# Taking out TensorE's transposes of the identity between the last attention product and the first gate product of a decoder layer

## What is computed

```python
def xattn(input, weight, bias):                 # input is x1, weight is ctx_2048
    x_dq = _fp8_quant_dequant(input)            # scale = 448 / max(abs(x1)), over ALL of x1
    w_dq = _fp8_quant_dequant(weight)
    return jnp.einsum('bmk,bkn->bmn', x_dq, w_dq) + bias

x = layernorm(x + attn(x))                      # x1
x = layernorm(x + xattn(x, ctx, mask))          # x2
x = layernorm(x + ffn(x))                       # silu(x @ gate_w) * (x @ up_w) @ down_w, and experts
```

## Time and profile before

| what | value |
|---|---|
| median of 3 executions | 802.43 us (802.11 to 802.63) |
| the profiled execution's own time | 802.24 us |
| its span, first to last instruction | 800.4 us |
| mean granted TensorE clock over the span | 0.996 |
| PE busy | 778.9 us, 97% of the span |
| DVE busy | 672.9 us, 84% |
| ACT, POOL busy | 317.4 us, 367.6 us |

### The profile page before, as it was taken

The page is one execution under the profiler, slowest core; times in us unless marked ns, Lnnn a source line. Parts: engine busy times, 40 slices in busy tenths (PEclk is TensorE's granted clock), DMA queues, the critical chain, the costliest instruction groups (busy, mean ns, idle before and its releaser), DMA issues. The chain is left out here.

```text
span 800.4 us, 10702 instructions
## 1 busy us (share of the span) xinstructions
PE 778.9 (97%) x3614; PEld 639.1 (80%) x3614; DVE 672.9 (84%) x1334; ACT 317.4 (40%) x696; POOL 367.6 (46%) x300
## 2 busy tenths in 40 slices
PE   8999999999899999999999999999999999999994
PEld 7888888888667878888888888888877877878783
DVE  6887679898889870567699999999999999999997
ACT  6444337365673422222534333333233342333323
POOL 1332122242123311033468767767667667667432
PEclk9999999999999999999999999999999999999998
DMA  8667505635455547001122322322233333322113
GB/s 318 234 146 171 106 9 126 156 89 91 75 132 132 132 119 248 1 1 61 47 62 81 90 74 82 87 81 58 89 110 86 98 84 112 92 65 72 29 53 157
DMA packets 51190, 81.16 MB, mean 101 GB/s; under 512 B 17503, under 2 KB 26463, under 8 KB 50624
## 3 DMA queue, kind: packets, MB, share of 16 engines
q0 software_dynamic: 24240, 32.96, 19.3%
q1 hardware_dynamic: 25312, 47.52, 16.9%
q10 hardware_dynamic: 1584, 0.01, 0.1%
HBM read 110.44 MB, written 12.58 MB: 154 GB/s over the span
## 5 line engine op out<-in xcount | busy, mean ns | idle before, releaser
L1806 PE MATMUL gu<-x_hi,w_hi 128*128 128x512 f32 x516 | 202.1, 392 | 1.8 <-ACT mid L1411 1.8
L1808 PE MATMUL gu<-x_hi,w_lo 128*128 128x512 f32 x516 | 200.8, 389 | 0.0
L1807 PE MATMUL gu<-x_lo,w_hi 128*128 128x512 f32 x516 | 200.8, 389 | 0.0
L1291 POOL TENSOR_TENSOR h_lo<-mid,h_hi 128x512 fp32r<-128x512 f32 x62 | 80.5, 1318 | 103.5 <-ACT h_hi L1417 103.0
L1427 ACT ACTIVATE gates<-dots 128x1 f32<-128x1 f32 x144 | 29.3, 203 | 232.2 <-DVE dots L1663 232.2
L1806 PEld LDWEIGHTS gu<-x_hi,w_hi 128*128 128x128 f32 x516 | 96.9, 188 | 24.0 <-ACT mid L1411 4.3
L1808 PEld LDWEIGHTS gu<-x_hi,w_lo 128*128 128x128 f32 x516 | 96.9, 188 | 20.3
L1807 PEld LDWEIGHTS gu<-x_lo,w_hi 128*128 128x128 f32 x516 | 96.9, 188 | 19.8
L1310 POOL DMA_INDIRECT ctx_q<-table_dram,row_i x64 | 80.3, 1254 | 62.3 <-DVE xall L1672 42.6
L1310 POOL DMA_INDIRECT scratch<-table_dram,row_i x64 | 82.4, 1287 | 39.9 <-issue 23.7
L1572 DVE TENSOR_TENSOR mid<-gu,mid 128x512 f32<-128x512 f32 x64 | 44.1, 690 | 62.3 <-PE gu L1808 41.1
(11 more groups left out here) (249 smaller groups left out, 1446.6 us busy)
## 6 DMA issues: line engine op xcount, KB each, us to landing
stage<-in_ctx SPq DMA_DIRECT2D x7, 1024.0 KB, 6.1
total<-prod POOLq DMA_DIRECT2D x11, 512.0 KB, 4.8
xall<-half_bo POOLq DMA_DIRECT2D x4, 1024.0 KB, 9.9
xhat<-in_L_ffn_gate_w SPq DMA_DIRECT2D x8, 512.0 KB, 3.4
xhat<-in_L_ffn_up_w SPq DMA_DIRECT2D x8, 512.0 KB, 3.4
xall<-in_mask_Bx1xS_ff POOLq DMA_DIRECT2D x4, 1024.0 KB, 10.5
xhat<-in_L_ffn_down_w SPq DMA_DIRECT2D x8, 512.0 KB, 3.4
x_dram<-xall SPq DMA_DIRECT2D x4, 1024.0 KB, 6.9
```

The lines of the kernel that those rows point to most:

```text
L1291: nc.gpsimd.tensor_tensor(lo[:, c], mid[c][:], hi[:, c].bitcast(F32), ALU.subtract).then_inc(hlo_done, 1)
L1806: nc.tensor.matmul(dst, lhs[0], rhs[0], start=start, stop=False)
L1807: nc.tensor.matmul(dst, lhs[0], rhs[1], start=False, stop=False)
L1808: return nc.tensor.matmul(dst, lhs[1], rhs[0], start=False, stop=stop)
```

## The change

All eight groups are taken out, and with them the waits that stood ahead of them. Of the waits, two kinds stay behind in another form: `largest_everywhere` now has a wait for `z_done` of tile 13 (NT - 3), the last reader of its bank `ob2`, ahead of its wait for the diagonal; the waits for `y_scaled`, `minus_first`, `y_done` (TB + 2) and `v3_ready` are gone from this place. No other instruction of any engine changes, and none changes its place.

```diff
@@ first block, PE @@
                 for i in range(TB):
                     attention(LAST, i)
 
-                def keep_running(count):
-
-                    for _ in range(count):
-                        nc.tensor.transpose(ob[3][:, 0:P], ident[:], ident[:])
-
-
-                pe.wait_ge(z_done, NT - 2)
-                keep_running(16)
-                pe.wait_ge(z_done, NT)
-                keep_running(8)
-                pe.wait_ge(x1_done, NT - 1)
-                keep_running(6)
+                pe.wait_ge(z_done, NT - 3)
                 largest_everywhere()
-                keep_running(10)
@@ second block, PE @@
-                def keep_running(bank, count):
-
-                    for _ in range(count):
-                        nc.tensor.transpose(bank[:, 0:P], ident[:], ident[:])
-
-
-                pe.wait_ge(y_scaled, 1)
-                keep_running(ob[3], 5)
                 for i in range(TB):
                     transposes(1, (i,), own_bank, x1t_mm, freed(y_done, 0))
                     cross(0, nothing, (i,))
-                pe.wait_ge(y_done, TB + 2)
-                for i in range(1, TB):
-                    pe.wait_ge(minus_first, i + 1)
-                    keep_running(gu[0], 7)
-                pe.wait_ge(v3_ready, 2)
-                keep_running(gu[0], 4)
                 x2_transposes(0, nothing)
-                keep_running(gu[0], 3)
                 for n in range(TB - 1):
                     gate_up(n, 0, n, 0, 2 if n == 0 else None)
```

## The result

| | kernel before | changed kernel |
|---|---|---|
| median of 20 executions | 802.67 us | 804.66 us |
| lowest to highest | 802.11 to 804.09 us | 802.92 to 809.21 us |
| ratio to before, 95% interval | | 1.0025 (1.0017 to 1.0034) |
| the profiled execution's own time, its span | 802.24, 800.4 us | 805.71, 803.9 us |
| mean granted clock over the span | 0.996 | 0.985 |

A forecast was written before the change was run, and what follows sets the result against it. PE bounds the kernel from the first gate product on, so its delay moves the end. The delay of 0.8 us, with the barrier's -0.2 already in it, on 802.43 gives 803.2 us; range 802.0 to 806.0.

The forecast's parts named there:

- The hidden transposes: The 73 identity transposes hide under the chain of DVE and ACT; their removal costed at nothing, except the ten behind L873.
- some 0.2 us at the barrier: Barrier after L873: without the ten transposes DVE arrives last, 0.20 us sooner: -0.2 us, bounds 0 and 0.49.
- The first fall: Clock halves at about 210.8 or later, cross products start at half speed; 2.4 us lost, 1.44 hidden, +0.8 us at end.
- the bound of +0.25: If L873 already runs at half speed, it ends 0.25 us later, on the chain to the scale: +0.25 us.
- The 4.9 us of slow running: Restart cost read from the program's beginning: 2.4 us lost, at half speed 4.9 us before the clock is up.
- The second fall: Rival: clock falls again, or isn't back, ahead of the gate products; +2.2 on top of +0.8, 805.4 us; chance 0.25.
- each of its gaps is under 4.8 us: Argument against another fall between 220.2 and 228: no gap reaches the idle time after which the clock fell at program's end.
- the share of work: Argument for a fall between 205.96 and 215.19: PE works only an eighth of 9.2 us, nearer to nothing than 44%.
- The likeliest case: One fall of the clock with most of its cost hidden: 803.2 us, within 802.4 to 804.0; chance 0.43.
- the case that had 0.35 against 0.62: Whole kernel slower by a tellable 1.6 us, 804.0 or more: chance 0.35; within that of no change: 0.62.
- Down throughout: Rival: clock stays down from 211 us until the gate products are well under way; +6.8 us, 809 us; chance 0.06.
- The page's rule: Rival from the skill page: transposes don't engage the full clock, so the 73 did nothing; 802.2 us; chance 0.04.

The follow-up runs named there:

- no_ten: The kernel before without only the ten transposes behind L873: 802.31 us against 802.58; the same kernel once more 802.87 against 802.51.
- six: The kernel before with six transposes behind L873 instead of ten: 802.28 us against 802.51, ratio 0.9995.
- second_only: The kernel before without the first block's groups (16, 8, 6, 10), the second block's kept: 802.90 us against 802.58, ratio 1.0000.
- only_sevens: The changed kernel with the three groups of seven back, between cross products and x2 transposes: 803.10 us against before's 802.65, ratio 1.0002.
- first_only: The kernel before without the second block's groups (5, 3 x 7, 4, 3), the first block's kept: 804.47 us against 802.58, ratio 1.0017.
- one_each: The kernel before with one transpose in each place, 10 in all instead of 73, all waits kept: 803.72 us against 802.58, ratio 1.0013.
- only_four_three: The changed kernel with only the groups of 4 and 3 around the x2 transposes back: 803.78 us against before's 802.51, ratio 1.0014.
- start_transposes: The kernel before with its first 16 products of zeros replaced by 32 transposes of the identity: 806.11 us against 802.51, ratio 1.0039.
- fuller: The kernel before with six transposes instead of ten behind L873 and two more thin places filled: 803.05 us against 802.65, ratio 1.0007.
- half_transposes: The kernel before with 30 transposes instead of 73, spread over all the places: 803.68 us against 802.65, ratio 1.0013.

## Why the prediction was right, and where it wasn't

**The hidden transposes.** Right. 73 transposes fed nothing, and taking them out gained nothing but some 0.2 us at the barrier (0.16 in the changed kernel, and 0.16 in no_ten and six without what was early ahead of it).

**The first fall.** Right in its place and nearly so in its size: forecast at 210.8 or somewhat later, in the profiled run at about 209.8. It came in every run, none having 0.996. It made the fourth residual 1.08 us late where 0.76 was forecast, and two errors partly cancel in that. The second block began 0.37 us late instead of 0.20 early, by L873 at half speed (the bound of +0.25) and a stage ahead that was 0.16 us later. From there to the end of the last cross product (222.70 against 220.22) PE lost 2.1 us instead of 2.4. The x2 transposes began at 225.24 (forecast 225.1). The 4.9 us of slow running were no constant: the clock was back at about 220.0 here, and at 218.0 in second_only, whose cross products begin at nearly the same time. By the medians the cost of this fall alone is 0.3 to 0.5 us in second_only and only_sevens, which isn't clear of no change, and the eight runs with one fall have a median of 803.3 where 803.2 was forecast.

**The second fall.** Its price was right in sum, and its chance was not. Worked out were 805.4 us; the ten runs of that group have a median of 805.6. The parts came out otherwise. I had all sixteen x2 transposes at half speed, ending 1.3 us late; they took 0.51 us more, since the clock fell only when PE had been at them for 1.6 us, and the twelve gate products behind took 2.30 us more. But I gave it 0.25, and it came in ten or eleven of 20 runs, and in seven of 11 of first_only. The step that failed is the argument against it: "each of its gaps is under 4.8 us". I had taken the 4.8 us between the last product and the fall at the end for a length that a gap must reach. one_each shows that none over 1.92 us is needed, no_ten falls with 1.95, and only_four_three fell 2.0 us after the last product. For the first stretch I had argued with the share of work; for the second, with the length of gaps. The second argument is refuted. That little work is what brings the clock down fits all rows, but they do not say how little: six falls with most of the filling in place. In the changed kernel the gap ahead of the x2 transposes is 2.54 us, and the clock fell at 226.9, when PE had been at them for 1.6 us. That the fall of a given kernel comes in some runs and not in others is what the rows show, and the prediction had no term for it.

**The likeliest case.** By the runs it was not clearly the likeliest: eight or nine runs to ten or eleven. The median, 804.66, lies at the edge between the two groups. It is inside the range of 802.0 to 806.0, because that took in the second fall, and above 803.2 by 1.5 us. That the median came no higher than this edge is luck of how the 20 runs divided. At 2.0 us over before it is also beyond the 1.6 us that I called tellable, the case that had 0.35 against 0.62.

**Down throughout.** Two of 20 runs are at 808.2 and 809.2, where 809 was worked out. The one at 809.2 has the lowest clock, 0.981, some 24 us at half. The one at 808.2 has 0.986, so its extra time is not the clock's alone. Neither has a profile, so the mechanism isn't shown.

**The page's rule.** The Trainium skill, "TensorE: Matmul & The Clock Gate", Part 4, has transposes not engage the full clock. By it the change would have done nothing but free the barrier. The measurement decides against it: in start_transposes 32 transposes alone bring the clock up after 5.6 us, and taking the 73 out brought it down in every run.

## What to carry to other kernels

A stretch in which PE has little to do costs nothing itself, but it may leave PE at half speed for the next 3 to 10 us. What that costs is decided by what runs then: under work with room (here the cross products, 1.44 us) the start of the x2 transposes came 0 to 0.9 us later, and in front of the unbroken chain of products a fall cost 0.9 us more (only_four_three, under the x2 transposes) to 2.8 us more (the changed kernel, under the gate products too). So filling is worth placing ahead of the unbroken work, in enough quantity, and away from barriers that it can hold up. And where runs fall in groups, look at the clock of each run before reading a median: two kernels with one median may be mixtures in other shares.

## What I had not expected of the hardware

- Filling with 30 of the 73 transposes is worth hardly more time than one transpose in each place: 1.03 and 1.14 us over before. Filling counts at its full length on the path once the clock has fallen: six transposes 1.49 us, where ten took 1.26 at full speed.
- The clock fell at 209.8 in the changed kernel and at 207.9 in only_four_three, 211.3 in one_each, 214.6 in no_ten and 212.9 in fuller. How long it then stayed down differed: some 10 us in the changed kernel, 7 in second_only and 3 in no_ten. More filling did not always bring it back sooner: 7 us in one_each, 10 in half_transposes.
- Products of the identity, 40 rows, hold the clock no better than 30 transposes of it (0.988 to 0.992 against 0.988 to 0.994).
